# Half of each sequence's first-pass scores moved from the feed-forward part into the sequence's own attention

## The reference

```
for L in range(4):                      # block 0 has a top-2-of-4 expert MLP, the others one MLP
    h = layernorm(x) * (1 + scale1) + shift1
    q, k, v = split(h @ w_qkv + b_qkv)  # 16 heads of 18
    x = x + gate1 * (softmax(q k^T / sqrt(18)) v) @ w_o + b_o      # gate1 on the whole of the projection
    h = layernorm(x) * (1 + scale2) + shift2
    x = x + gate2 * (gelu(h @ w1 + b1) @ w2 + b2)                  # hidden width 1152
```

## Time and profile before

| what | value |
|---|---|
| median of 3 runs | 2216.1 us (2212.15 to 2219.96) |
| the profiled execution | 2227.37 us |
| its span, first to last instruction | 2225.6 us |
| PE busy | 2023.0 us (91%) |
| DVE busy | 1336.7 us (60%) |
| ACT busy | 1143.4 us (51%) |
| mean granted PE clock | 0.939 |

### The profile page before, as it was taken

One profiled execution on the slowest core, in us unless ns is written; L12 is line 12 of the kernel. 1 busy time (PEld: TensorE's weight loads), 2 busy tenths in 40 slices (PEclk: granted clock), 3 DMA queues, 4 the chain that ended last, 5 costly groups with the idle time before them and its releaser, 6 DMA issues.

```text
span 2225.6 us, 38981 instructions
## 1 busy us (share of the span) xinstructions
PE 2023.0 (91%) x15592; PEld 1502.7 (68%) x15592; DVE 1336.7 (60%) x2940; ACT 1143.4 (51%) x1705; POOL 208.2 (9%) x311
## 2 busy tenths in 40 slices
PE   6988999899998999999899899998997898999998
PEld 4346478748974896698475556887886646474658
DVE  4747647656674677576657582462545858584832
ACT  2353734474555465555726555553344463737363
POOL 2000111111110210011020000001100000000001
PEclk9586999899999999999989999998899999999999
DMA  5234241343234232523331412446155141414111
GB/s 162 56 118 85 72 124 56 75 110 94 72 78 138 60 90 52 141 85 81 97 89 18 123 7 65 69 80 129 33 101 115 25 126 23 102 13 113 17 10 25
DMA packets 204731, 173.97 MB, mean 78 GB/s; under 512 B 54822, under 2 KB 164678, under 8 KB 204550
## 3 DMA queue, kind: packets, MB, share of 16 engines
q1 hardware_dynamic: 197974, 158.76, 30.7%
q0 software_dynamic: 6576, 12.71, 2.1%
HBM read 125.57 MB, written 40.11 MB: 74 GB/s over the span
## 4 chain that ended last, share of the span: by engine, by line
PE 63%; DVE 18%; ACT 11%; DMA 3%; issue 2%; SPq 2%; POOL 0%; ACTq 0%; POOLq 0%; DVEq 0%
PE PSA L1881 16%; PE PSA L1896 14%; DVE MX L1520 8%; PE PSA L1671 5%; PE PSA L1785 5%; PE PSA L1762 5%; ACT PB L1369 4%; PE PSA L1732 4%; PE PSA L1775 4%; PE PSA L1744 2%; PE PSA L1805 1%; DVE HH L1650 1%; PE PSA L1694 1%; ACT FH L1399 1%; DVE FL L1420 1%
## 5 line engine op out<-in xcount | busy, mean ns | idle before, releaser
L1520 DVE TENSOR_REDUCE MX<-PSA 128x1 f32<-128x512 f32 x768 | 490.2, 682 | 289.5 <-PE PSA L1762 285.9
L1881 PE MATMUL PSA<-A,FH 128*128 128x256 f32 x2520 | 444.6, 292 | 14.6 <-DVE HH L1650 10.4
L1896 PE MATMUL PSA<-FH,HH 128*128 128x288 f32 x2016 | 447.9, 313 | 3.3 <-DVE HH L1650 3.3
L1406 ACT ACTIVATE HH<-PSA 128x512 fp32r<-128x512 f32 x252 | 150.6, 598 | 565.0 <-PE PSA L1881 555.5
L1369 ACT ACTIVATE PB<-PSA 128x1024 f32<-128x1024 f32 x384 | 371.0, 1025 | 103.8 <-PE PSA L1775 103.0
L1881 PEld LDWEIGHTS PSA<-A,FH 128*128 128x128 f32 x2520 | 364.9, 195 | 37.1 <-issue 18.6
L1896 PEld LDWEIGHTS PSA<-FH,HH 128*128 128x128 f32 x2016 | 329.0, 195 | 45.1 <-issue 38.5
L1896 PE MATMUL PSA<-FL,HH 128*128 128x288 f32 x1008 | 303.4, 301 | 0.0
L1762 PE MATMUL PSA<-KS,QS 54*128 54x512 f32 x768 | 227.2, 513 | 35.1 <-DVE MX L1520 14.7
L1274 POOL TENSOR_TENSOR X<-X,TM 128x288 f32<-128x288 f32 x128 | 101.3, 809 | 1476.3 <-DVE TM L1585 1476.2
L1785 PE MATMUL PSA<-PB,VT 128*32 128x512 f32 x1536 | 221.9, 643 | 0.0
(11 more groups left out here) (171 smaller groups left out, 2252.4 us busy)
## 6 DMA issues: line engine op xcount, KB each, us to landing
qkd<-HH SPq DMA_DIRECT2D x48, 504.0 KB
ST<-in_L_cond_w SPq DMA_DIRECT2D x51, 432.0 KB
ST<-in_L_cond_w SPq DMA_DIRECT2D x102, 192.0 KB
QS<-qkd SPq DMA_DIRECT2D x88, 144.0 KB
KS<-qkd SPq DMA_DIRECT2D x88, 144.0 KB
QS<-qkd SPq DMA_DIRECT2D x144, 72.0 KB
KS<-qkd SPq DMA_DIRECT2D x144, 72.0 KB
ST<-in_L_cond_w SPq DMA_DIRECT2D x153, 48.0 KB
```

What stands on the lines that cost most here:

```text
L1406: e.activation(r(HH[u][:, 0, :]), PS[bk][:, :], gelu)
L1520: e.reduce_max(MX[p // 2 % 2][:, col:col + 1], PS[bk][:, :], axis=AX.X).then_inc(free[bk], 1)
L1881: m = e.matmul(PS[bk][:, s_ * 256:(s_ + 1) * 256], r(w_), r(x_[:, half * 256:(half + 1) * 256]), start=(z == 0), stop=(z == 6))
L1896: m = e.matmul(PS[bk][:, 0:C], r(HH[u][:, c, tk]), r(w_), start=False, stop=(j == NCH - 1 and z == 2))
```

## The change

Groups 2 and 3 (`g >= HELD`) of sequence i are not stepped until `at_steps(i)` has begun; what is left late of group 1 (its `rows`) is put out first. In attention i two first-pass visits are stepped per attention step until the `rows` of group 3 of i have been put out, then one. No instruction is added or taken away; instructions of lines 1520, 1526, 1529, 1762, 1768 and 1129 change place in the list. Sequence 0 was stepped so already, and block 2 has another first pass.

```diff
@@ -35,6 +35,7 @@
 BG = 3
+HELD = 2
 TURN_AT = 2
@@ -399,7 +400,7 @@
-    hurry, stream = [False], []
+    hurry, stream, at_now = [False], [], [-1]
@@ -422,6 +423,13 @@
         late = None
         for p in range(H // 2):
             g = p // 2
+            if g >= HELD and at_now[0] != i:
+                if late is not None:
+                    yield
+                    rows(*late)
+                    late = None
+                while at_now[0] != i:
+                    yield
             for q in range(QT):
@@ -449,6 +457,7 @@
     def at_steps(i):
         exps = {}
+        at_now[0] = i
@@ -457,7 +466,7 @@
-            for _ in range(2 if i == 0 else 1):
+            for _ in range(2 if i == 0 or s1_at[0] < (i, 3) else 1):
                 s1_step()
```

## The result

The changed kernel took 2332.22 us (median of 4 runs, 2324.89 to 2339.22) against 2218.03 for the kernel before on the same chip: a ratio of 1.0516, 95% interval 1.0472 to 1.056, or +114 us where +42 was forecast. The sign was right; the time lies above the range.

What follows compares the result with a forecast made beforehand. PE was taken to bound the four-expert gaps and DVE the first half of attention. Costs of 69 + 5 + 31 + 2 = 107 us less 65 us gain gave +42: 2258, rounded down to 2256 us, range 2210 to 2300.

Steps and rivals of the forecast that it cites:

- The sign: Whole kernel: slower than before, by 42 us; slower by more than 6.6 us was given 0.77.
- Where the visits go: Attention's first six steps: 53 visits become 121; of 107 moved, 68 land there and 39 in steps 6 to 8.
- The gain of the gaps: Gaps between attentions: 214 matmuls leave, giving back 65 us, between 59 and 79.
- DVE's time in the first six steps: Eleven attentions: DVE's need rises from 152.2 to 236.5 us and limits these steps, costing 69 us.
- slower by the clock: Rival, first eight steps of touched attentions: lower PE clock, 88 us more, 2345 us; chance 0.1 for most of this.
- the sum: Whole kernel: 69 + 5 + 31 + 2 = 107 us of cost against 65 us of gain, +42 us.
- A busy DVE alone doesn't lower it: Argument on PE's clock: sequence 4's first half ran at 1.00 with DVE busy 14.52 of 15.3 us.
- its price, 3.18 us: Two-visit attention step: takes at least 3.18 us at full clock, read from sequence 0 in the trace.
- Steps 6 to 8: Attention steps 6 to 8: 39 moved visits at 0.8 us each cost 31 us, between 17 and 38.
- The queues passed: Attention: group 3's rows are issued in step 9, behind qkin loads for most sequences; +2 us in sum.
- The faster rival: Rival: PE sets the pace, attention's steps 9 to 12 catch up; cost 58 us, about 2202 us; chance 0.13.
- the wash: Rival: attention's cost is near 70 us, kernel at 2211 to 2224 us; chance 0.12.

Runs made afterwards that it cites:

- e9: The changed kernel with no group held back, two visits a step in attention kept: 2253.0 us, ratio 1.013.
- e4: The changed kernel with each first-pass maximum taken over 256 of its 512 columns: 2209.88 us, ratio 0.9986.
- e1: The changed kernel with the second visit of an attention step issued after the step's av matmuls instead of before: 2264.71 us, ratio 1.0209.
- e8: The changed kernel with only group 3 held back and one visit a step: 2196.05 us, ratio 0.9907.
- e10: The changed kernel with groups 2 and 3 still held back but one visit a step: 2420.88 us, ratio 1.0885.
- e11: e8 with its one visit a step placed behind av instead of before it: 2246.8 us, ratio 1.0116.
- e3: The changed kernel with the first matmul of a step's second visit issued two extra times, in 7 visits a sequence: 2329.63 us, ratio 1.0525.

## Why the prediction was wrong

**Where the visits go** was right: 121 in the first six steps, eleven in each (22 weight loads of line 1771 in each of the eleven windows; the first and last and the sum stand below), against 121 forecast.

```profile
221.50:247.50 26.00, 8.55 (x22) 4.17 (x22) 0.80 0.11 33
...
2203.50:2225.60 22.10, 8.32 (x22) 4.14 (x22) 0.77 0.28 33
sum 282.30, PE 95.33 PEld 46.59; mean PE 8.67 PEld 4.24
```

**The gain of the gaps** was right: 67.0 us, 65 forecast. Part of it is luck: the clock lost in the eleven gaps fell from 80 to 69 us, 8 of the 11 in the gap that holds block 2, and at 0.7 to 0.9 this is 8 to 10 us. The visits themselves gave 57 to 59, the low end.

**DVE's time in the first six steps** was right (228.41 us, 236.5 forecast), but not that it is the limit. DVE would be over 90% busy, the prediction said; it is at 81%, and in the step shown it waits for PE. e9 agrees: 36 us more DVE time made 62 us more.

**The step that failed** is the rival "slower by the clock", given 0.1 and left out of the sum, whose terms for the visits stand at full clock. "A busy DVE alone doesn't lower it" is true of the earlier trace rows, but the change adds more than busy DVE: PE's waits in every two-visit step. Clock lost over the eleven attentions: 12 us before and 63 after in the first six steps, 0 and 44 in steps 6 to 8. At 0.68 to 0.76 and 0.89 that is 35 to 39 and 39, so 74 to 78 us, worked out from rows of e4 and e1. The attentions took 182 - 107 = 75 us more than forecast. A second working needs no such price, though it rests on PE's modelled busy time. In these nine steps that time rose by 144.4 us and PE's idle time by 40.1. The moved matmuls account for 58 of the busy time at 0.27 us each, so the other 86 are the same work taking longer. The sum's 107 us held the same 58 and 49 of waits: the waits were no worse than forecast, and the slower PE is what the sum lacked. The rival's own price was 88, its time 2345; measured 2332. It also named the right signs, steps of 5 us and `qk` tiles at half speed: sequence 13's tile in the timeline above takes 2.07 us for its first four matmuls, 1.20 before the change.

The falls were there to be seen. The earlier trace rows show sequence 0 doing the very step that the change brings to eleven more attentions, at 0.51 for 18 us. The prediction took its price, 3.18 us, from the part at full clock, and the rest as a rival. A step seen at two prices in one trace belongs in the sum at a weight.

**Steps 6 to 8** were forecast at +31 and took +80: 39 by clock as above, the rest, some 41, bank waits and work (PE's idle time there rose by 17.8 us). e1, with av over the wait, took +27.9 there. The prediction allowed a visit 0.55 us of wait for DVE's maxima, and missed that the second visit waits for the `qk` tile's bank, which ACT and DVE both have to read (1.98 us in the row shown). Of DVE's order it counted only that the low parts of the turned rows come later; that the reading of the tile's own bank stands behind the maxima too was not in it.

**The queues passed** (+2): line 1784 waited 11.2 us for the rows' DMAs against 8.3, +2.9.

**The faster rival and the wash** are out: PE did not catch up in steps 9 to 15, which took 227.3 us (229.7 before).

The Trainium skill, page "TensorE: Matmul & The Clock Gate", section "What's actually happening", has activity release the throttle. For the fall, the trace agrees: it came after waits of PE, at the gap's end and in the two-visit steps. For the return it doesn't: sequence 3's first six steps in e4 had 0.59 on the mean with PE shown busy for 26.45 of 29.20 us. What keeps the clock down there is open; no run could set the clock by itself, so its share is worked out from rows, not measured by taking it away. What the runs show by taking it away is the cause in the program: two visits a step, with av queued behind the second.

## What to carry to other kernels

Before work is moved to a place where PE will wait for a bank or an engine, price it at both clocks: find that step in the trace at each, and ask which will be granted. Spreading such work one piece a step helped here only while it was done before its reader needed it (e8, not e10), and other matmuls over the wait helped with two pieces a step (e1), not with one (e11). In a ring of few banks count every reader that must let go before the next fill, not the slowest engine alone, and ask what stands ahead of each reading in its engine's order.

## What the runs showed of the hardware that was not expected

In one execution the first six steps of two attentions, each with 104 matmuls and with DVE and ACT busy alike within 0.21 us, took 19.30 us at a granted clock of 1.00 and 27.80 at 0.60 (e4, sequences 7 and 6): 44% more. PE can be shown over 90% busy and stay at the lower level for most of such a stretch. And two more matmuls put into each of PE's waits (e3) halved its idle time in these steps and gave back only 11 of the 63 us of clock lost.
